# Attention: the causal mask of the transposed scores, by matrix products or by a selection on GpSimd

## The chip, the cores and the metric

The kernel runs on one core of one Trainium2 chip. The metric is the device time of one execution in microseconds (us). Before the change three runs gave 3653.22, 3657.49 and 3666.11 us; the median is 3657.49 us.

## The reference, cut to what matters

The whole program is a two-layer network on 16 sequences of 512 tokens with 128 features. The change touches one part of layer 0, where two attentions run on the same normalised input: A, without a causal mask (with a decay by distance), and B, causal. Both have 16 heads of 8 features. For B:

```python
scores = jnp.einsum('bhqd,bhkd->bhqk', q, k) / jnp.sqrt(jnp.float32(HD))
causal = jnp.tril(jnp.ones((s, s), dtype=bool))
scores = jnp.where(causal, scores, -jnp.inf)
attn = jax.nn.softmax(scores, axis=-1)
y = jnp.einsum('bhqk,bhkd->bhqd', attn, v)
```

The heads' outputs go on to a projection, a mixture of experts and a second layer, which the change does not touch.

## The kernel before, in words

`program` runs its stages one after the other: `fold_weights` (loads and reshapes weights), `front` (normalisation and projections), `attend` (both attentions of all heads), `tail`, `route`, `experts`, then layer 1. Only `fold_weights` and `attend` are changed.

`attend` works on 16 x 16 = 256 heads, one per step of a loop written out in full, and in groups of four heads. Keys come in four blocks of 128 (j = 0 to 3), queries are 512 wide. For each head there are three families of score products on TensorE (PE):

- A0 to A3: the scores of attention A, transposed (keys on partitions, queries along the free dimension), 512 wide each (line 627). VectorE (DVE) multiplies the first (j+1) x 128 columns by a decay ratio, in place in PSUM (line 782); ScalarE (ACT) takes the exponential into `pA` (line 729).
- M0, M1, M2: the scores of attention B with queries on partitions (line 633; M0 has the two narrow blocks, M1 the 384 wide one, M2 the 512 wide one). DVE takes the causal maximum of every row (line 791). Once per group these maxima are transposed (job MT, line 676), negated by DVE (line 754), split into three bfloat16 parts by GpSimd (POOL, lines 609 to 612), and loaded by DMA as three more rows of the operand `bq`.
- T0, T1, T2: the scores of attention B, transposed, eight steps after M (LAG = 8), because they need the maxima (line 640; T0 has key block 0, 512 wide; T1 has blocks 1 and 3, 384 and 128 wide; T2 has block 2, 256 wide). Behind each of the four products a second one, of the identity with `cmaskT`, adds -1e30 above the diagonal of the block's first 128 columns (line 643). ACT takes the exponential into `pB` (line 735), which has six slots.

Once per group the values are multiplied in: PV of A has four chunks, one for each key block (eight matmul records per chunk, 512 wide), PV of T has chunks 0 (512 wide), 1 (384 wide) and 2 with 3 (256 and 128 wide together) (line 659). ACT then copies the sum from PSUM (`copy`, line 718), PE transposes it (jobs OT, line 672), and DVE divides by the softmax sum (lines 762 and 764).

What sets the order: three hand-written sequences, one for each engine, in which every step's work is issued.

```python
BANK = dict(A0=2, A1=4, A2=0, A3=1, M0=5, M1=4, M2=3, T0=5, T1=3, T2=2)
PE_ORDER = ("T0", "M2", "A0", "at0", "A1", "A3", "T1", "at1", "M0", "A2", "T2", "at2", "M1")
ACT_ORDER = (("copy", 1), ("T1", 1), ("T2", 1), ("A3", 1), ("A2", 1), ("copy", 0), ("T0", 0), ("A0", 0), ("A1", 0))
DVE_ORDER = ("M2", "A0", "A1", "job", "A3", "M0", "A2", "M1")
```

The number in `ACT_ORDER` says how many steps late ACT does the piece. Two score families share each PSUM bank but two (bank 0 for A2, bank 1 for A3), and a product waits until the bank's previous occupant has been read (`free_bank`, line 616). The once-a-group work goes into the places at0, at1 and at2 of PE's order. A planner (lines 495 to 513) puts it there by a number q counted from the first step e of a group (e divisible by 4): q goes to step e + q // 3, place at(q mod 3). Before: PV of T at q = 2, 3, 4, its transpose at 9; PV of A at 7, 8, 10, 12, its transpose at 17 (which is place at2 of step 1 of the next group); MT at 2. In the texts "step 0" to "step 3" are the steps with e mod 4 = 0 to 3. The PSUM bank of the values is copied by ACT in the same step if the last chunk was at at0 ("copy", 0) and first thing in the next step if it was at at1 or at2 ("copy", 1).

Of the kernel before, what the change touches and what calls it, by code (L numbers as in the profile page):

```python
# [18 lines left out]
BF16 = mybir.dt.bfloat16  # L19
I32 = mybir.dt.int32  # L20
U32 = mybir.dt.uint32
ALU = mybir.AluOpType
# [3 lines left out]
P = 128  # L26
NB, S, D = 16, 512, 128
# [11 lines left out]
MASKED = -1e30  # L39
# [19 lines left out]
def fold_weights(nc, c, W):  # L59

    with ExitStack() as ctx:
        sb = lambda n, s, d=F32: ctx.enter_context(nc.sbuf_tensor(n, s, d))
        sem = lambda n: ctx.enter_context(nc.semaphore(n))
        wk, wv, wsum, wsumT = sb("fw_k", [P, D]), sb("fw_v", [P, D]), sb("fw_s", [P, D]), sb("fw_sT", [P, D])
        wd, wuk, wuv = sb("fw_d", [P, 32]), sb("fw_uk", [32, D]), sb("fw_uv", [32, D])
        bT = sb("fw_bT", [32, D])
        wqkv, wqkv_g, g1 = sb("fw_qkv", [P, 3 * D]), sb("fw_qkv_g", [P, 3 * D]), sb("fw_g1", [P, 1])
        wq, cmaskT = sb("fw_q", [P, D]), sb("fw_cmaskT", [P, P])
        ps = ctx.enter_context(nc.psum_tensor("fw_ps", [P, 4, 512], F32))
        s_in, s_sum, s_pe, s_cp = sem("fw_in"), sem("fw_sum"), sem("fw_pe"), sem("fw_cp")  # L70
        block = ctx.enter_context(nc.Block())
        loads = [(wk, c["Wk"]), (wv, c["Wv"]), (wd, c["Wdown"]), (wuk, c["Wuk"]), (wuv, c["Wuv"]),
                 (wqkv, c["Wqkv"]), (g1, c["g1"]), (wq, c["Wq"]), (W["woA"], c["WoA"]), (W["woB"], c["WoB"]),
                 (W["ident"], c["ident"]), (W["hsum"], c["hsum"]), (cmaskT, c["cmaskT"]),
                 (W["ratio"], c["ratio"]), (W["cmask"], c["cmask"]), (W["g2b"], c["g2b"]), (W["wr"], c["Wr"])]

        by_head = lambda ap: ap.rearrange("p (h d) -> p h d", d=HD)
        by_feature = lambda ap: ap.rearrange("p (d h) -> p h d", d=HD)

        @block.sync  # L80
        def _(sp):
            for dst, src in loads:
                sp.dma_start(dst[:], src).then_inc(s_in, 16)

        @block.vector
        def _(dve):
            dve.wait_ge(s_in, 16 * len(loads))
            dve.tensor_tensor(wsum[:], wk[:], wv[:], ALU.add).then_inc(s_sum, 1)

            dve.tensor_scalar(wqkv_g[:], wqkv[:], g1[:, 0:1], None, ALU.mult).then_inc(s_sum, 1)  # L90
            dve.tensor_copy(by_feature(W["wqA"][:]), by_head(wq[:]))
            dve.tensor_copy(W["ident_bf"][:], W["ident"][:])
            dve.tensor_copy(W["cmaskT"][:], cmaskT[:])
            dve.memset(W["mhalf"][:], -0.5)
            dve.wait_ge(s_sum, 2)
            dve.tensor_copy(W["wB"][:, 2 * D:3 * D], wqkv_g[:, 2 * D:3 * D])
            for t in range(2):
                src = by_head(wqkv_g[:, t * D:(t + 1) * D])
                dve.tensor_copy(by_feature(W["wB"][:, t * D:(t + 1) * D]), src)

                pairs = src.rearrange("p h (n two) -> p h n two", two=2)
                dst = by_feature(W["wB"][:, (3 + t) * D:(4 + t) * D]).rearrange("p h (n two) -> p h n two", two=2)
                dve.tensor_copy(dst[:, :, :, 0], pairs[:, :, :, 1])
                dve.tensor_copy(dst[:, :, :, 1], pairs[:, :, :, 0])
            dve.wait_ge(s_pe, 1)
            dve.tensor_copy(wsumT[:], ps[:, 0, 0:D]).then_inc(s_cp, 1)
            dve.wait_ge(s_pe, 2)
            dve.tensor_copy(bT[:], ps[0:32, 1, 0:D]).then_inc(s_cp, 1)
            dve.wait_ge(s_pe, 4)
            dve.tensor_copy(by_feature(W["mk"][:]), by_head(ps[:, 2, 0:D]))  # L110
            dve.tensor_copy(W["mv"][:], ps[:, 3, 0:D]).then_inc(s_cp, 1)
            dve.wait_ge(s_cp, 3)

        @block.tensor
        def _(pe):
            pe.wait_ge(s_sum, 1)
            pe.transpose(ps[:, 0, 0:D], wsum[:], W["ident"][:]).then_inc(s_pe, 1)
            pe.wait_ge(s_cp, 1)

            pe.matmul(ps[0:32, 1, 0:D], wd[:], wsumT[:], start=True, stop=True).then_inc(s_pe, 1)  # L120
            pe.wait_ge(s_cp, 2)
            pe.matmul(ps[:, 2, 0:D], bT[:], wuk[:], start=True, stop=True).then_inc(s_pe, 1)
            pe.matmul(ps[:, 3, 0:D], bT[:], wuv[:], start=True, stop=True).then_inc(s_pe, 1)
# [296 lines left out]
def attend(nc, c, W, nb):  # L420
# [4 lines left out]
    with ExitStack() as ctx:  # L425
        sb = lambda n, s, d=F32: ctx.enter_context(nc.sbuf_tensor("at_" + n, s, d))
        sem = lambda n: ctx.enter_context(nc.semaphore("at_" + n))
# [22 lines left out]
        stored = [[sem(f"stored{a}{n}") for n in range(2)] for a in range(2)]  # L450
        filled, tilted, maxed, exped = (sem(n) for n in "filled tilted maxed exped".split())
        pv, ot_cp, job, job_read, m_ready = (sem(n) for n in "pv ot_cp job job_read m_ready".split())
        v_step, p_step, ones = (sem(n) for n in "v_step p_step ones".split())

        BANK = dict(A0=2, A1=4, A2=0, A3=1, M0=5, M1=4, M2=3, T0=5, T1=3, T2=2)
        PE_ORDER = ("T0", "M2", "A0", "at0", "A1", "A3", "T1", "at1", "M0", "A2", "T2", "at2", "M1")
# [41 lines left out]
        for e in range(0, STEPS):  # L498
            if e % 4 == 0 and e >= 4:
                if 0 <= (e - 4 - LAG) // 4 < GROUPS:  # L500
                    g = (e - 4 - LAG) // 4
                    for q, chunks in ((2, (0,)), (3, (1,)), (4, (2, 3))):
                        put(e, q, ("PV", "T", g, chunks))
                    put(e, 9, ("OT", "T", g))
                if (e - 4) // 4 < GROUPS:
                    g = (e - 4) // 4
                    for j, q in enumerate((7, 8, 10, 12)):
                        put(e, q, ("PV", "A", g, (j,)))
                    put(e, 17, ("OT", "A", g))
                    put(e, 2, ("MT", "M", g))  # L510
# [6 lines left out]
        jseq = {j: n for n, j in enumerate(jobs)}  # L517
        pvseq = {g: n for n, g in enumerate(pv_order)}
        LAST = 1 + max(e for (e, n), w in plan.items() if w)

        last_head = {"A": "A2", "T": "T2"}

        with nc.Block() as block:

# [69 lines left out]
            @block.gpsimd  # L594
            def _(pool):
                step = [0]

                def link(ins):

                    step[0] += 1  # L600
                    ins.then_inc(p_step, 1)
                    pool.wait_ge(p_step, step[0])

                for n in range(GROUPS):
                    b = n % 2
                    pool.wait_ge(job_read, jseq["MT", "M", n] + 1)
                    if n >= 2:
                        pool.wait_ge(m_in[(n - 2) % B_GROUPS], 48 * ((n - 2) // B_GROUPS + 1))
                    link(pool.tensor_copy(mrow[:, b, 0], neg[:, b]))  # L609
                    link(pool.tensor_tensor(res[:, b], neg[:, b], mrow[:, b, 0], ALU.subtract))  # L610
                    link(pool.tensor_copy(mrow[:, b, 1], res[:, b]))
                    pool.tensor_tensor(mrow[:, b, 2], res[:, b], mrow[:, b, 1], ALU.subtract).then_inc(m_ready, 1)

            @block.tensor
            def _(pe):
# [21 lines left out]
                def scores_t(kind, n):  # L637
                    slot = n // 4 % B_GROUPS
                    for j, col in T_BLOCKS[kind]:
                        pe.matmul(ps[:, BANK[kind], col:col + S - j * P], bk[:, slot, n % 4, j * P:(j + 1) * P], bq[:, slot, n % 4, j * P:S],  # L640
                                  start=True, stop=False)

                        ins = pe.matmul(ps[:, BANK[kind], col:col + P], W["ident_bf"][:], W["cmaskT"][:], start=False, stop=True)  # L643
                    ins.then_inc(filled, 1)

                def values(kind, g, chunks):
                    a, b = "AT".index(kind), g // NG
                    if chunks[0] == 0:
                        pe.wait_ge(v_in[b % 2], 32 * (b // 2 + 1))
                        pe.wait_ge(exped, nth["exped", (last_head[kind], 4 * g + 3)])  # L650
                        if pvseq[kind, g]:
                            pe.wait_ge(ot_cp, pvseq[kind, g])
                    for j in chunks:
# [1486 lines left out]
def weights(nc, ctx):  # L2140
# [2 lines left out]
                  ratio=[P, S], cmask=[P, S], hsum=[P, H], g2b=[P, D], wr=[P, E], mhalf=[P, 2 * NC],  # L2143
                  nmax=[H, 2 * NB])
    W = {n: sb(n, s) for n, s in shapes.items()}
    W["ident_bf"], W["cmaskT"], W["flag"] = sb("ident_bf", [P, P], BF16), sb("cmaskT", [P, P], BF16), sb("flag", [1, 1], I32)
    return W


def shape_constants():  # L2150
# [6 lines left out]
    cmask[:, S - P:] = np.where(np.arange(P)[None, :] <= np.arange(P)[:, None], 0.0, MASKED)  # L2157

    hsum = (np.arange(P)[:, None] % H == np.arange(H)[None, :]).astype(f32)
    cmaskT = np.where(np.arange(P)[:, None] <= np.arange(P)[None, :], 0.0, MASKED).astype(f32)  # L2160
    theta = (f32(10000.0) ** (f32(-2.0) * (np.arange(HD // 2, dtype=f32) / HD))).astype(f32)
    ang = (pos[:, None] * theta[None, :]).astype(f32)
    feature = np.arange(P) // H
# [22 lines left out]
    i, j = np.arange(P)[:, None] % SEG, np.arange(SEG)[None, :]  # L2186
    scan = dict(cos1=per_side(cos1), sin1=per_side(sin1), mask1=np.where(j <= i, 0.0, MASKED).astype(f32))
    return dict(**route, **scan, ident=np.eye(P, dtype=f32), decay=decay, ratio=ratio, cmask=cmask,
                hsum=hsum, cmaskT=cmaskT, rope=rope)


def inputs_of(a):
# [56 lines left out]
```

## Time and profile before

| | us |
|---|---|
| runs (three): median (lowest to highest) | 3657.49 (3653.22 to 3666.11) |
| the profiled execution, its own time | 3638.61 |
| its span from first to last instruction | 3636.5 |
| `attend`, first score product to last division | about 397 to 1600 |
| PE busy over the span | 2978.0 (82%) |
| DVE busy | 2830.2 (78%) |
| ACT busy | 1774.0 (49%) |
| POOL busy | 1734.2 (48%) |

The span covers all stages; shares of it say little of one stage. A PE matmul's record has a modelled end and overlaps its neighbours, so PE's work is read from the spacing of starts rather than from the busy share.

### The profile page before, as it was taken

How to read it: one execution, taken by the hardware profiler on the slowest of the kernel's cores; microseconds unless marked ns; L12 is line 12 of the kernel's file. 1: busy time of each engine (PE TensorE's matmuls, PEld its weight loads, DVE VectorE, ACT ScalarE, POOL GpSimd, SP SyncE). 2: the span in 40 equal slices, each digit the busy share in tenths (PEclk: the TensorE clock that was granted, in tenths of full speed). 3: DMA queues.
4: the chain of work that ended last, by engine and by line, in shares of the span. 5: the costliest groups of instructions: out<-in, count | busy, mean ns of one | idle time of the engine just before them, and what ended most of it. 6: DMA issues, size and time to landing. Idle time of an engine off the chain costs nothing. (4 is left out here: it accounts for less than half of the span.)

```text
span 3636.5 us, 134756 instructions
## 1 busy us (share of the span) xinstructions
PE 2978.0 (82%) x56132; PEld 1772.6 (49%) x56132; DVE 2830.2 (78%) x7779; ACT 1774.0 (49%) x3541; POOL 1734.2 (48%) x1622
## 2 busy tenths in 40 slices
PE   4554599999999999985054179999999999999999
PEld 2222133333333333355012057777777777777777
DVE  5777788888888888857883578888888888888886
ACT  2222477787888877751000044444444444444443
POOL 4555000000000000012004478888888888888886
PEclk9777699999999999997565589999999999999999
DMA  3444533333333333247001300000000000000000
GB/s 129 147 152 153 131 78 79 81 86 82 81 84 86 86 81 81 71 127 226 3 0 34 80 9 10 10 10 10 10 10 10 10 7 7 10 10 10 10 7 10
DMA packets 179124, 210.76 MB, mean 58 GB/s; under 512 B 28196, under 2 KB 139876, under 8 KB 178276
## 3 DMA queue, kind: packets, MB, share of 16 engines
q1 hardware_dynamic: 175972, 200.94, 20.0%
q8 instruction: 442, 7.24, 0.9%
q0 software_dynamic: 2560, 1.35, 0.3%
q14 instruction: 150, 1.23, 0.1%
HBM read 125.79 MB, written 75.63 MB: 55 GB/s over the span
## 5 line engine op out<-in xcount | busy, mean ns | idle before, releaser
L729 ACT ACTIVATE at_pA<-at_ps 128x512 f32<-128x512 f32 x1024 | 569.4, 608 | 134.0 <-DVE at_ps L782 133.3
L791 DVE CUSTOM_DVE_ANT_0 at_junk<-at_ps,w_cmask 128x512 f32<-128x512 f32 (+3 forms) x1024 | 462.3, 487 | 166.4 <-PE at_ps L633 166.4
L609 POOL CAST at_mrow<-at_neg 16x128 bf16<-16x128 f32 x64 | 18.0, 281 | 1106.6 <-DVE at_neg L754 1106.6
L782 DVE TENSOR_TENSOR at_ps<-at_ps,w_ratio 128x128 f32<-128x128 f32 (+3 forms) x1024 | 490.0, 493 | 65.5 <-PE at_ps L627 65.4
L2001 ACT ACTIVATE sc_ee<-sc_ps 128x512 f32<-128x512 f32 x256 | 153.1, 598 | 606.2 <-PE sc_ps L1856 602.0
L735 ACT ACTIVATE at_pB<-at_ps 128x512 f32<-128x512 f32 (+1 forms) x768 | 395.9, 539 | 75.9 <-PE at_ps L643 73.0
L1819 POOL TENSOR_TENSOR sc_rb<-sc_rb,v_sin 128x512 f32<-128x512 f32 x256 | 326.2, 1274 | 99.6 <-DVE sc_ra L2040 99.1
L627 PE MATMUL at_ps<-at_aq,at_ak 72*128 72x512 bf16 x1024 | 353.3, 388 | 3.2 <-DMA at_ak<-parts_scratch 2.8
L1856 PE MATMUL sc_ps<-sc_xT,v_wqkv 128*128 128x512 f32 x512 | 298.4, 666 | 50.1 <-DVE sc_ra L2040 48.7
L633 PE MATMUL at_ps<-at_bk,at_bq 72*128 72x512 bf16 (+3 forms) x1024 | 271.3, 307 | 57.0 <-DMA at_bk<-parts_scratch 35.8
L640 PE MATMUL at_ps<-at_bq,at_bk 75*128 75x512 bf16 (+3 forms) x1024 | 281.4, 301 | 18.7 <-DVE at_mx L791 17.7
L659 PE MATMUL at_ps<-at_pA,at_v 128*32 128x512 f32 x2048 | 275.5, 610 | 0.0
L1881 PE MATMUL sc_ps<-v_uu,sc_skN 32*64 32x65 f32 x8192 | 259.6, 226 | 4.8 <-issue 1.3
L1881 PEld LDWEIGHTS sc_ps<-v_uu,sc_skN 32*64 32x64 f32 x8192 | 223.0, 135 | 52.3 <-issue 46.3
L2050 DVE TENSOR_TENSOR v_mem<-v_mem,sc_ps 128x520 f32<-128x520 f32 x256 | 171.9, 672 | 66.3 <-PE sc_ps L1881 66.3
L633 PEld LDWEIGHTS at_ps<-at_bk,at_bq 72*128 72x128 bf16 x1024 | 80.1, 99 | 280.4 <-ACT at_pA L729 123.6
L643 PE MATMUL at_ps<-w_cmaskT,w_ident_bf 128*128 128x128 bf16 x1024 | 198.3, 219 | 0.0
L2039 DVE STREAM_SHUFFLE sc_rb<-sc_ps 128x512 f32<-128x512 f32 x256 | 187.6, 733 | 0.0
L1933 PE MATMUL sc_ps<-v_wout,sc_oT 128*128 128x128 f32 x1024 | 183.6, 303 | 0.6
L1814 POOL TENSOR_TENSOR sc_sq<-sc_ee,sc_relu 128x512 f32<-128x512 f32 x128 | 165.1, 1290 | 36.6 <-ACT sc_ee L2004 36.2
L1814 POOL TENSOR_TENSOR sc_sk<-sc_ee,sc_relu 128x512 f32<-128x512 f32 x128 | 163.0, 1273 | 35.9 <-ACT sc_ee L2004 35.2
L659 PE MATMUL at_ps<-at_pB,at_v 128*32 128x512 f32 (+3 forms) x2048 | 177.3, 442 | 1.3 <-issue 0.9
(299 smaller groups left out, 6620.4 us busy)
## 6 DMA issues: line engine op xcount, KB each, us to landing
parts_scratch<-fr_parts SPq DMA_DIRECT2D x64, 384.0 KB, 2.8
at_bq<-parts_scratch SPq DMA_DIRECT2D x192, 96.0 KB
at_bk<-parts_scratch SPq DMA_DIRECT2D x192, 96.0 KB
at_aq<-parts_scratch SPq DMA_DIRECT2D x192, 96.0 KB
at_ak<-parts_scratch SPq DMA_DIRECT2D x192, 96.0 KB
v_scratch<-fr_v SPq DMA_DIRECT2D x32, 352.0 KB, 2.3
at_v<-v_scratch SPq DMA_DIRECT2D x32, 352.0 KB, 3.6
parts_scratch<-fr_parts SPq DMA_DIRECT2D x32, 256.0 KB, 2.8
```

What stands on the lines that cost most here:

```text
L627: pe.matmul(ps[:, BANK[f"A{j}"], :], ak[:, slot, n % 4, j * P:(j + 1) * P], aq[:, slot, n % 4], start=True, stop=True).then_inc(filled, 1)
L633: ins = pe.matmul(ps[:, BANK[kind], col:col + wide], bq[0:ROWS, slot, n % 4, j * P:(j + 1) * P], bk[0:ROWS, slot, n % 4, 0:wide], start=Tr ...
L640: pe.matmul(ps[:, BANK[kind], col:col + S - j * P], bk[:, slot, n % 4, j * P:(j + 1) * P], bq[:, slot, n % 4, j * P:S], start=True, stop=F ...
L659: ins = pe.matmul(ps[32 * s:32 * s + 32, PV, q0:S], v[:, b % 2, a, j, h * (HD + 1):h * (HD + 1) + 32], probs, start=(j == 0), stop=(j == N ...
L729: act.activation(pA[:, n % A_RING, j * S:(j + 1) * S], src, ACT.Exp).then_inc(exped, 1)
L735: act.activation(pB[:, n % T_RING, at:at + wide], src[:, 0:wide], ACT.Exp).then_inc(exped, 1)
L782: dve.tensor_tensor(src[:, 0:wide], src[:, 0:wide], W["ratio"][:, S - wide:S], ALU.mult).then_inc(tilted, 1)
L791: ins = dve.tensor_tensor_reduce(junk[:, P * j * (j + 1) // 2:P * (j + 1) * (j + 2) // 2], src[:, col:col + wide], W["cmask"][:, S - wide: ...
L1814: pool.tensor_tensor(sig[which][:, p % 4], ee[:, n % 2], relu[:, n % 2], ALU.add).then_inc(G["sg"], 1)
L1819: pool.tensor_tensor(by_pos(rb[:, n % 2]), by_pos(rb[:, n % 2]), table("sin", which), ALU.mult).then_inc(G["sn"], 1)
L1856: pe.matmul(ps[:, bank_of("qk"[which], p), :], V["wqkv"][:, col:col + P], xT[:, p // PAIRS % 2], start=True, stop=True).then_inc(G["pj"], 1)
L1881: ins = pe.matmul(ps[64 * hh:64 * hh + 64, 4 + f % 2, g * VE:(g + 1) * VE], skN[32 * f:32 * f + 32, p % 4, g, 64 * hh:64 * hh + 64], uu[32 ...
```

## The change

It leaves out the four identity products per head, and the constant `cmaskT` with its load and two casts. After the exponentials of T1 and T2 have been taken, POOL sets to 0, in `pB`, the entries whose query index within the diagonal block is below the key index: one selection over 128x128 (block 3) after T1 and one over three 128x128 blocks (0, 1 and 2) after T2, for each head. PE's products of the values wait for a new semaphore, `cut`, in place of the exponential. The planner's places of PV of T move from q = 2, 3, 4 to 3, 4, 5, and its transpose from 9 to 10. POOL's splitting of the maxima is now issued between the selections.

```diff
-            dve.tensor_copy(W["ident_bf"][:], W["ident"][:])
-            dve.tensor_copy(W["cmaskT"][:], cmaskT[:])
...
-                    for q, chunks in ((2, (0,)), (3, (1,)), (4, (2, 3))):
+                    for q, chunks in ((3, (0,)), (4, (1,)), (5, (2, 3))):
                         put(e, q, ("PV", "T", g, chunks))
-                    put(e, 9, ("OT", "T", g))
+                    put(e, 10, ("OT", "T", g))
...
-                for n in range(GROUPS):
+                def split_max(n):
...
+                def cut_future(n):
+
+                    probs = pB[:, n % T_RING]
+                    pool.wait_ge(exped, nth["exped", ("T1", n)])
+                    lone = probs[:, B_AT[3]:B_AT[3] + P]
+                    pool.affine_select(lone, lone, [[1, P]], ALU.is_ge, 0.0, base=0, channel_multiplier=-1).then_inc(cut, 1)
+                    pool.wait_ge(exped, nth["exped", ("T2", n)])
+                    three = bass.AP(probs.tensor, probs.offset, [list(probs.ap[0]), [S, 3], [1, P]])
+                    pool.affine_select(three, three, [[0, 3], [1, P]], ALU.is_ge, 0.0, base=0, channel_multiplier=-1).then_inc(cut, 1)
+
+                for e in range(STEPS):
+                    n = head_of("T", e)
+                    if n is not None:
+                        cut_future(n)
+                    if e % 4 == 0 and 0 <= e // 4 - 1 < GROUPS:
+                        split_max(e // 4 - 1)
...
                     for j, col in T_BLOCKS[kind]:
-                        pe.matmul(ps[:, BANK[kind], col:col + S - j * P], bk[:, slot, n % 4, j * P:(j + 1) * P], bq[:, slot, n % 4, j * P:S],
-                                  start=True, stop=False)
-
-                        ins = pe.matmul(ps[:, BANK[kind], col:col + P], W["ident_bf"][:], W["cmaskT"][:], start=False, stop=True)
+                        ins = pe.matmul(ps[:, BANK[kind], col:col + S - j * P], bk[:, slot, n % 4, j * P:(j + 1) * P], bq[:, slot, n % 4, j * P:S],
+                                        start=True, stop=True)
...
-                        pe.wait_ge(exped, nth["exped", (last_head[kind], 4 * g + 3)])
+                        if a == 0:
+                            pe.wait_ge(exped, nth["exped", ("A2", 4 * g + 3)])
+                        else:
+                            pe.wait_ge(cut, 2 * (4 * g + 3) + 2)
```

## Rows read from the trace of the kernel before

**Rows 1.** Busy time of a stretch of `attend`: PE, PEld, DVE, ACT, POOL, clock, DMA.
```profile
900.00:1000.00 100.00, 96.92 (x743) 39.31 (x744) 81.22 (x291) 80.39 (x165) 7.42 (x21) 1.00 0.31 74
```

**Rows 2.** Waits between 500 and 1500 us: total us, times, longest us.
```profile
PEld at_ps L627 <- DVE at_mx L791: 99.2, 162, 0.8
...
ACT at_oT L718 <- PE at_ps L659: 61.3, 108, 0.9
```

**Rows 3.** PE in time over one group: start us, us, what, [idle before <-releaser].
```profile
882.16 0.38 PE L640 MATMUL at_ps<-at_bq,at_bk 75*128 75x512 bf16 x1
...
883.61 0.34 PE L640 MATMUL at_ps<-at_bq,at_bk 75*128 75x384 bf16 x1
...
886.88 0.38 PE L640 MATMUL at_ps<-at_bq,at_bk 75*128 75x512 bf16 x1
...
891.06 0.38 PE L640 MATMUL at_ps<-at_bq,at_bk 75*128 75x512 bf16 x1 [0.28 <-DVE at_mx L791]
891.28 0.22 PE L643 MATMUL at_ps<-w_cmaskT,w_ident_bf 128*128 128x128 bf16 x1
891.34 0.38 PE L633 MATMUL at_ps<-at_bk,at_bq 72*128 72x512 bf16 x1
891.55 0.38 PE L627 MATMUL at_ps<-at_aq,at_ak 72*128 72x512 bf16 x1
891.86 1.07 PE L659 MATMUL at_ps<-at_pA,at_v 128*32 128x512 f32 x8
892.86 0.60 PE L627 MATMUL at_ps<-at_aq,at_ak 72*128 72x512 bf16 x2
...
894.13 0.34 PE L633 MATMUL at_ps<-at_bk,at_bq 72*128 72x128 bf16 x2 [0.33 <-ACT at_pB L735]
...
896.17 0.38 PE L640 MATMUL at_ps<-at_bq,at_bk 75*128 75x512 bf16 x1
...
898.63 0.86 PE L659 MATMUL at_ps<-at_pB,at_v 128*32 128x256 f32 x16
899.42 0.34 PE L633 MATMUL at_ps<-at_bk,at_bq 72*128 72x128 bf16 x2
...
899.99 0.61 PE L672 MATMUL at_ps<-w_ident,at_oT 128*128 128x128 f32 x4
900.43 0.33 PE L633 MATMUL at_ps<-at_bk,at_bq 72*128 72x384 bf16 x1
900.60 0.38 PE L640 MATMUL at_ps<-at_bq,at_bk 75*128 75x512 bf16 x1
```

**Rows 4.** ACT in time, the same group.
```profile
892.99 0.59 ACT L718 COPY at_oT<-at_ps 128x512 f32<-128x512 f32 x1 [0.91 <-PE at_ps L659]
893.48 0.60 ACT L735 ACTIVATE at_pB<-at_ps 128x512 f32<-128x512 f32 x1
...
899.56 0.59 ACT L718 COPY at_oT<-at_ps 128x512 f32<-128x512 f32 x1 [0.25 <-PE at_ps L659]
```

**Rows 5.** DVE in time, the same group.
```profile
890.49 0.42 DVE L791 CUSTOM_DVE_ANT_0 at_junk<-at_ps,w_cmask 128x256 f32<-128x256 f32 x1
890.83 0.09 DVE L791 DVE_READ_ACCUMULATOR2_ANT at_mx<- 128x1 f32 x1
...
893.63 0.24 DVE L762 RECIPROCAL at_rr<-at_ps 128x16 f32<-128x16 f32 x1
...
894.12 0.69 DVE L782 TENSOR_TENSOR at_ps<-at_ps,w_ratio 128x512 f32<-128x512 f32 x1
894.71 0.28 DVE L791 CUSTOM_DVE_ANT_0 at_junk<-at_ps,w_cmask 128x128 f32<-128x128 f32 x1
```

**Rows 6.** POOL: groups by line and shape, busy us and mean ns.
```profile
L1819 POOL TENSOR_TENSOR sc_rb<-sc_rb,v_sin 128x512 f32<-128x512 f32 x256 | 326.2, 1274 | 99.6 <-DVE sc_ra L2040 99.1
...
L226 POOL TENSOR_TENSOR fr_sc<-fr_sc,w_mhalf 128x8 f32<-128x8 f32 x8 | 13.4, 1671 | 0.7
...
L1518 POOL MEMSET v_mem<- 128x8320 f32 x1 | 7.0, 7039 | 0.0
```

More of the change, by code:

```diff
@@ L67, in fold_weights @@
         wqkv, wqkv_g, g1 = sb("fw_qkv", [P, 3 * D]), sb("fw_qkv_g", [P, 3 * D]), sb("fw_g1", [P, 1])
-        wq, cmaskT = sb("fw_q", [P, D]), sb("fw_cmaskT", [P, P])
+        wq = sb("fw_q", [P, D])
         ps = ctx.enter_context(nc.psum_tensor("fw_ps", [P, 4, 512], F32))
@@ L73, in fold_weights @@
                  (wqkv, c["Wqkv"]), (g1, c["g1"]), (wq, c["Wq"]), (W["woA"], c["WoA"]), (W["woB"], c["WoB"]),
-                 (W["ident"], c["ident"]), (W["hsum"], c["hsum"]), (cmaskT, c["cmaskT"]),
+                 (W["ident"], c["ident"]), (W["hsum"], c["hsum"]),
                  (W["ratio"], c["ratio"]), (W["cmask"], c["cmask"]), (W["g2b"], c["g2b"]), (W["wr"], c["Wr"])]
@@ L452, in attend @@
         pv, ot_cp, job, job_read, m_ready = (sem(n) for n in "pv ot_cp job job_read m_ready".split())
-        v_step, p_step, ones = (sem(n) for n in "v_step p_step ones".split())
+        v_step, p_step, ones, cut = (sem(n) for n in "v_step p_step ones cut".split())
         BANK = dict(A0=2, A1=4, A2=0, A3=1, M0=5, M1=4, M2=3, T0=5, T1=3, T2=2)
@@ L519, in attend @@
         LAST = 1 + max(e for (e, n), w in plan.items() if w)
-        last_head = {"A": "A2", "T": "T2"}
         with nc.Block() as block:
@@ L2145, in weights @@
     W = {n: sb(n, s) for n, s in shapes.items()}
-    W["ident_bf"], W["cmaskT"], W["flag"] = sb("ident_bf", [P, P], BF16), sb("cmaskT", [P, P], BF16), sb("flag", [1, 1], I32)
+    W["flag"] = sb("flag", [1, 1], I32)
     return W
@@ L2159, in shape_constants @@
     hsum = (np.arange(P)[:, None] % H == np.arange(H)[None, :]).astype(f32)
-    cmaskT = np.where(np.arange(P)[:, None] <= np.arange(P)[None, :], 0.0, MASKED).astype(f32)
     theta = (f32(10000.0) ** (f32(-2.0) * (np.arange(HD // 2, dtype=f32) / HD))).astype(f32)
@@ L2188, in shape_constants @@
     return dict(**route, **scan, ident=np.eye(P, dtype=f32), decay=decay, ratio=ratio, cmask=cmask,
-                hsum=hsum, cmaskT=cmaskT, rope=rope)
+                hsum=hsum, rope=rope)
 def inputs_of(a):
```

## The prediction

> **What bounds it now.** I began with the page's busy shares and its 40 slices, which set `attend` apart (about 397 to 1600 us), then took the stretch table for a hundred microseconds of it [rows 1]. There TensorE's granted clock is 1.00 of 2.4 GHz; DVE and ACT are busy 81 and 80 of 100 us, POOL 7. PE's 97 is modelled. So no engine is plainly full, and POOL has room. The wait table [rows 2] shows each engine waiting for another: PE for DVE's maxima (99.2 us in 1000), ACT's copy for PE's values (61.3 us, 108 times, thus twice in each of 54 groups). What bounds the stage is a chain that runs through three in-order engines and the shared PSUM banks, so I laid out one group in time.
>
> The T0 products open the steps: 882.16, 886.88, 891.06, 896.17, 900.60 [rows 3]. Step 2 takes 4.72 us, step 3 4.18, step 0 5.11, step 1 4.43: 18.44 us for four heads. Starts are spaced by the columns: a mask product takes 0.06 us (891.28 to 891.34), a 512-wide score 0.21 to 0.22, a chunk of values 1.00 (891.86 to 892.86), or 0.79 for T's chunks 2 and 3 (898.63 to 899.42; chunk 1 likewise), and a transpose job 0.44 (899.99 to 900.43). On ACT a 512-wide piece costs 0.49 (892.99 to 893.48) and is ready at 0.60 [rows 4]. On DVE A3 costs 0.59, and M0's maximum is ready at 890.92, whereupon PE's T0 starts at 891.06 [rows 5].
>
> Followed in time, PE is the chain from T1 of step 2 (883.61) to step 0, except for a DVE piece before 891.06. In step 0 the values of A end at 892.86, ACT copies at 892.99, takes T0's exponential from 893.48, and only then PE's M0 starts (894.13) [rows 3, 4]. PE carries it again to M0 at 899.42. From there to the T1 that corresponds to 883.61, 2.63 us, it is DVE: M0, A2, M1 and M2 in sequence.
>
> **Part 1: the mask products.** Sixteen per group go, each 0.058 us of PE. Eleven lie on the chain: T1's two in each of steps 1, 2 and 3, T0's one in steps 0, 1 and 3, T2's one in steps 0 and 2. The other five are covered: in step 0 T1's two by ACT's copy, in steps 1 to 3 T2, T0 and T2 by DVE. 11 x 0.058 = 0.64 us per group; 62 groups with both kinds of values make 40 us. This alone would be a gain. The page "TensorE: Matmul & The Clock Gate" of the Trainium skill, section Back-to-back issue gap, gives about 81 ns per 128-column product in a stream with weight loads; by that the gain would be 11 x 0.081 x 62 = 55 us. The measured spacing decides: 0.058.
>
> **Part 2: POOL's selections.** The trace has none. Nearest rows [rows 6]: a memset writes 8320 elements in 7.04 us, 0.85 ns each (lower bound: 512 elements and two starts of 0.1, 0.6 us per head); a two-input operation over 512 takes 1.27, about 2.1 ns each over a start of 0.2; the power over 8 elements takes 1.67, 183 ns each (upper bound, 94 us per head). A selection is plain streaming work, so I take the two-input row: 0.45 + 0.99 = 1.45 us per head, inside a step of 4.6. The last head's T2 exponential ends before step 0's T0 plus 0.1 us; its second selection is done by 1.2, and its values are asked for at 5.03 (below). It costs nothing up to about 4.4 us per head, where POOL, with 1.4 us per group for splitting the maxima, would fill the step. POOL's splitting waits behind the next group's first selection; its result is due a whole group later.
>
> **Part 3: the moved values.** PV of T goes from place at2 of step 0 and at0, at1 of step 1 to at0, at1, at2 of step 1. I lay the group out again, masks gone, counting from step 0's T0 (0.00), waits as in the code:
> - Step 0: A0 0.42, values A3 0.73 to 1.72, A1, A3, T1 2.15. ACT copies at 1.85, T0's exponential ends 2.94, M0 2.99. DVE divides (OT of T) until 2.99, A3 until 3.56, M0 until 4.20. T0 of the next step: 4.30. Before it was 5.11: PV T0 (1.0) is gone, and DVE sets the end.
> - Step 1: A0 4.73, values T0 5.03 to 6.02, A1, A3, T1 6.45, values T1 6.76 to 7.55, M0 7.55, A2, T2 7.94, OT of A 8.05, values T2 and T3 8.54 to 9.33, M1, next T0 9.50. It is PE throughout: 5.20 against 4.43.
> - Step 2: the sum is now ready at 9.33, after T2 rather than before M0, and ACT's sequence has the copy ahead of T1's exponential, which has been ready since 7.0. Copy 9.46, T1's exponential 9.95 to 10.55; M2 needs its bank: 10.60 (PE idle for 0.9). DVE's M2 is ready at 11.71, T1 11.77, values A0 12.08, M0 13.07, values A1 13.66 to 14.65, next T0 14.82. 5.32 against 4.72: before, the copy and the exponential were done while PE still did M0, A2, T2, OT, M1 and T0.
> - Step 3: at0 is empty, so A1 waits for DVE's M1 (15.65) and T1 for M2 (16.24). OT of T 16.50, values A2 17.00 to 17.99, M0, DVE ready 19.01, next T0 19.15. 4.33 against 4.18.
>
> Sum: 4.30 + 5.20 + 5.32 + 4.33 = 19.15 against 18.44, 0.71 more. So the move costs 0.71 + 0.64 = 1.35 per group and gives back more than the masks bring. 62 x 0.71 = 44 us. At the start one DMA issue (0.47) and two casts (0.3) go; at the end the last values come a place later, about 1 us: nothing in all.
>
> The sum stands against the profiled execution's own 3638.61 us (span 3636.5): 3682.6. That execution was 18.9 us faster than the median 3657.49, to which the forecast refers: 3657.5 + 44 = **3701.5 us**.
>
> **Rivals.**
> - *The masks decide* (faster): ACT and DVE have slack of a fifth, and if my copy-and-exponential stall at step 2 is absorbed, 0.64 per group is won: 3657.5 - 40 = 3617. It turns at a cost of the move of 0.64 us per group. For: equal work moved within one group, POOL idle. Against: rows 3 and 4 show just this stall, 1.27 us from the end of values to M0, wherever a copy stands before an exponential that PE needs. 0.17.
> - *Gain and cost cancel*: the move costs about 0.64, half of what I laid out: 3657 give or take 11. 0.13.
> - *POOL becomes the bound*: beyond 4.4 us per head. At 5.0 a step is 5.0 + 0.35 = 5.35 instead of 4.61, on some 250 steps +185 us: 3842. For: POOL's rows span 0.85 to 183 ns per element. Against: 2.1 for everything streamed. 0.05. The page "GPSIMD Engine Reference", section Elementwise — side-by-side cycle accounting, says that data-dependent branching costs about 12 cycles per element; at its 1.2 GHz that would be 5.1 us per head and this rival's case. The selection depends on position and not on data, and no row here shows that price.
> - *The change doesn't do what it says*: the selected entries, 128 columns from each block's start with index below the partition's, are exactly those that `cmaskT` covered, so the work left is the same; I give this nothing.
>
> **Numbers.** The forecast's case has 0.65. Its own range: each step of the layout may be off by 0.1 to 0.15, 0.5 per group, so 0.2 to 1.3 per group, 3670 to 3738. For 8 in 10 I go down to 3630, which takes in the cancelling case and part of the faster one, and up to 3745; left out are most of the faster rival, POOL's case, and a tail. What a measurement can tell from no change is 0.3%, 11 us. From the cases: faster 0.19, same 0.13, slower 0.68.
>
> **What would show it.** In the changed profile: mask rows gone; T0 spaced 4.3, 5.2, 5.3, 4.3; 52 groups in 1000 us; ACT's idle before the copies about 2.9 us per group (0.9 before A's, 2.0 before T's) against 1.2; PE's M2 in step 2 waiting for T1's exponential; selections of 0.4 and 1.0 us, POOL busy about 35 in 100, PE never waiting for `cut`; DVE durations unchanged. I am wrong if M2 in step 2 follows T0 at once, if POOL's spacing per head passes 4 us, or if values of T start late behind `cut`.

## The result, and the profile after

The changed kernel takes 3716.83 us in the median of four runs (3710.63 to 3725.30), the kernel before 3655.35 in four; the ratio is 1.0166, with a 95% interval of 1.0131 to 1.0201. So it is 61 us slower; 3701.5 was forecast, in a range of 3630 to 3745.

The span of the profiled execution went from 3636.5 to 3709.5 us, 73 more. The work in `attend` went from 397.4 to 1599.8 us (first score product to the end of the last division) before, and from 395.6 to 1663.8 after: 1202.4 became 1268.3, 66 of the 73. What remains lies outside `attend`, in stages that the change does not touch but for the load and the two casts left out at the start. They took 2434.1 us of the span before and 2441.2 after; in the other profiles of this study they took between 2431 and 2453, so it is read as scatter.

First the stretch table of the changed kernel, with the columns of [rows 1] (PE, PEld, DVE, ACT, POOL, clock, DMA), over the same hundred microseconds:

```profile
900.00:1000.00 100.00, 91.69 (x623) 30.22 (x624) 77.16 (x277) 76.98 (x158) 23.84 (x62) 1.00 0.35 86
```

POOL went from 7 to 24 busy microseconds in 100, and PE, DVE and ACT all do less per microsecond than before: 277 DVE records against 291 (PE's fall also holds the mask products that are gone). The stage slowed as a whole, no engine became full, and the granted clock is still 1.00, the 2.4 GHz level. The groups of POOL in `attend` (busy us, mean ns) show why POOL is not the reason:

```profile
L618 POOL TENSOR_SCALAR_AFFINE_SELECT at_pB<-at_pB 128x384 f32<-128x384 f32 x256 | 133.3, 521 | 64.4 <-ACT at_pB L749 64.3
...
L615 POOL TENSOR_SCALAR_AFFINE_SELECT at_pB<-at_pB 128x128 f32<-128x128 f32 x256 | 74.8, 292 | 748.4 <-ACT at_pB L749 748.4
```

Together 0.81 us per head where 1.45 was taken, and inside a step of 4.8. It is POOL that waits, for ACT's exponentials. The waits between 500 and 1500 us, of which [rows 2] show two before:

```profile
ACT at_oT L732 <- PE at_ps L673: 144.5, 103, 2.6
PEld at_ps L646 <- ACT at_pB L749: 141.0, 155, 1.2
PEld at_ps L640 <- DVE at_mx L805: 110.7, 153, 0.8
```

ACT's idle before the copies of the value sums rose from 61.3 to 144.5 us, 2.8 per group (2.9 was expected). No product of values (L673) waits for a selection anywhere in the table. PE in time shows one group as the prediction laid it out; T0, 128x512 on line 653, opens each step:

```profile
901.25 0.39 PE L653 MATMUL at_ps<-at_bq,at_bk 75*128 75x512 bf16 x1
...
901.72 0.39 PE L640 MATMUL at_ps<-at_aq,at_ak 72*128 72x512 bf16 x1
902.04 1.07 PE L673 MATMUL at_ps<-at_pB,at_v 128*32 128x512 f32 x8
...
903.79 0.85 PE L673 MATMUL at_ps<-at_pB,at_v 128*32 128x384 f32 x8
904.58 0.34 PE L646 MATMUL at_ps<-at_bk,at_bq 72*128 72x128 bf16 x2
...
905.08 0.60 PE L686 MATMUL at_ps<-w_ident,at_oT 128*128 128x128 f32 x4
905.61 0.86 PE L673 MATMUL at_ps<-at_pB,at_v 128*32 128x256 f32 x16
906.40 0.34 PE L646 MATMUL at_ps<-at_bk,at_bq 72*128 72x384 bf16 x1
906.58 0.38 PE L653 MATMUL at_ps<-at_bq,at_bk 75*128 75x512 bf16 x1
907.68 0.39 PE L646 MATMUL at_ps<-at_bk,at_bq 72*128 72x512 bf16 x1 [0.72 <-ACT at_pB L749]
...
908.86 0.39 PE L653 MATMUL at_ps<-at_bq,at_bk 75*128 75x384 bf16 x2
...
911.95 0.38 PE L653 MATMUL at_ps<-at_bq,at_bk 75*128 75x512 bf16 x1
...
913.62 0.61 PE L686 MATMUL at_ps<-w_ident,at_oT 128*128 128x128 f32 x4
914.15 1.07 PE L673 MATMUL at_ps<-at_pA,at_v 128*32 128x512 f32 x8
...
916.32 0.38 PE L653 MATMUL at_ps<-at_bq,at_bk 75*128 75x512 bf16 x1 [0.34 <-DVE at_mx L805]
...
920.61 0.39 PE L653 MATMUL at_ps<-at_bq,at_bk 75*128 75x512 bf16 x1
```

And ACT around the long wait:

```profile
903.99 0.60 ACT L743 ACTIVATE at_pA<-at_ps 128x512 f32<-128x512 f32 x1 [0.35 <-DVE at_ps L796]
906.54 0.59 ACT L732 COPY at_oT<-at_ps 128x512 f32<-128x512 f32 x1 [1.95 <-PE at_ps L673]
907.02 0.88 ACT L749 ACTIVATE at_pB<-at_ps 128x512 f32<-128x512 f32 x2
```

Step by step, from T0 to T0 (before from [rows 3]):

| | before | laid out | measured |
|---|---|---|---|
| step 0 | 5.11 | 4.30 | 4.29 |
| step 1 | 4.43 | 5.20 | 5.33 |
| step 2 | 4.72 | 5.32 | 5.37 |
| step 3 | 4.18 | 4.33 | 4.37 |
| group | 18.44 | 19.15 | 19.36 |

ACT idles 1.95 us for T's sum, whose last product comes only after OT and just before M1; T1's exponential follows at 907.02; and PE's M2, whose bank T1 held, starts at 907.68, 1.10 after T0 where products go at 0.21 to 0.25. A group takes 0.92 us more than before.

### The profile page after: what moved, and what is told of

It reads as the page before. It is cut to its first block and busy times, and to the rows that moved or that the text cites. A ratio compares the mean times of both kernels' runs of the same rounds, so it can differ in the third digit from the quotient of the medians.

```text
span 3709.5 us, 133219 instructions
## 1 busy us (share of the span) xinstructions
PE 2987.7 (81%) x55108; PEld 1694.3 (46%) x55108; DVE 2829.3 (76%) x7777; ACT 1774.4 (48%) x3541; POOL 1939.1 (52%) x2134
## 3 DMA queue, kind: packets, MB, share of 16 engines
q0 software_dynamic: 2560, 1.35, 0.3%
## 5 line engine op out<-in xcount | busy, mean ns | idle before, releaser
L743 ACT ACTIVATE at_pA<-at_ps 128x512 f32<-128x512 f32 x1024 | 579.4, 615 | 109.8 <-DVE at_ps L796 108.6
L615 POOL TENSOR_SCALAR_AFFINE_SELECT at_pB<-at_pB 128x128 f32<-128x128 f32 x256 | 74.8, 292 | 748.4 <-ACT at_pB L749 748.4
L749 ACT ACTIVATE at_pB<-at_ps 128x512 f32<-128x512 f32 (+1 forms) x768 | 404.4, 551 | 58.2 <-PE at_ps L653 45.9
L653 PE MATMUL at_ps<-at_bq,at_bk 75*128 75x512 bf16 (+3 forms) x1024 | 269.2, 304 | 26.5 <-DVE at_mx L805 20.8
L673 PE MATMUL at_ps<-at_pA,at_v 128*32 128x512 f32 x2048 | 277.2, 613 | 0.0
L673 PE MATMUL at_ps<-at_pB,at_v 128*32 128x512 f32 (+3 forms) x2048 | 179.9, 447 | 1.2 <-issue 1.2
L640 PEld LDWEIGHTS at_ps<-at_aq,at_ak 72*128 72x128 bf16 x1024 | 80.5, 99 | 204.1 <-DVE at_mx L805 139.6
```

The costliest lines, as they stand in the source:

```text
L640: pe.matmul(ps[:, BANK[f"A{j}"], :], ak[:, slot, n % 4, j * P:(j + 1) * P], aq[:, slot, n % 4], start=True, stop=True).then_inc(filled, 1)
L673: ins = pe.matmul(ps[32 * s:32 * s + 32, PV, q0:S], v[:, b % 2, a, j, h * (HD + 1):h * (HD + 1) + 32], probs, start=(j == 0), stop=(j == N ...
L743: act.activation(pA[:, n % A_RING, j * S:(j + 1) * S], src, ACT.Exp).then_inc(exped, 1)
L749: act.activation(pB[:, n % T_RING, at:at + wide], src[:, 0:wide], ACT.Exp).then_inc(exped, 1)
```

## The experiments

Group times below are the distances of the first of POOL's splittings of the maxima, once per group. In the undisturbed stretches of a kernel nearly all of them agree to 0.02 us, so they resolve far more than the total time does. Each ratio is to runs of the kernel before that were taken beside the experiment; their medians lie between 3643 and 3655 us, so totals of different experiments are compared by their ratios.

**1. The selections without the move.** The changed kernel with

```diff
-                    for q, chunks in ((3, (0,)), (4, (1,)), (5, (2, 3))):
+                    for q, chunks in ((2, (0,)), (3, (1,)), (4, (2, 3))):
...
-                    put(e, 10, ("OT", "T", g))
+                    put(e, 9, ("OT", "T", g))
```

> The selections on POOL and no mask products, but the values of T and their transpose at their places of before (q = 2, 3, 4 and 9). Theory (the places cost, the masks bring): a group takes 18.44 - 0.64 = 17.8 us and the whole about 3655 - 40 = 3615 us. First rival (the selections or the wait for cut cost): the time stays near that of the changed kernel, 3717, and PE waits for POOL. Second rival (masks were covered): 3655.

Measured: 3609.63 us, ratio to before 0.9900 (0.9878 to 0.9921); group 17.79 to 17.80. The gain of 0.64 per group is, to 0.01, the eleven mask products on the chain times 0.058, and no value product waits for POOL:

```profile
915.19 0.38 PE L653 MATMUL at_ps<-at_bq,at_bk 75*128 75x512 bf16 x1 [0.34 <-DVE at_mx L805]
...
918.91 1.07 PE L673 MATMUL at_ps<-at_pB,at_v 128*32 128x512 f32 x8
```

The values of T start 3.72 us into step 0. POOL's last selection of that group (below) ends at 915.24 + 0.52 = 915.76, 3.15 us earlier. The old places had room for it.

```profile
915.24 0.52 POOL L618 TENSOR_SCALAR_AFFINE_SELECT at_pB<-at_pB 128x384 f32<-128x384 f32 x1 [0.43 <-ACT at_pB L749]
```

**2. The move without the selections.** The kernel before with the same lines of the planner changed the other way (2, 3, 4 to 3, 4, 5; 9 to 10).

> The kernel before, mask products and all, with only the places of T's values and transpose moved (q = 3, 4, 5 and 10). Theory: the move alone costs 1.35 to 1.55 us per group, so a group of 19.8 to 20.0 us and a time of 3655 + 84 to + 96, 3740 to 3750. Rival (the selections cost): near 3655.

Measured: 3743.66 us, ratio 1.0273 (1.0248 to 1.0298); group 19.93. The move costs 1.49 us per group with the masks and 19.36 - 17.80 = 1.56 without, where 1.35 was laid out. Here too the M2 of step 2 waits, with no selection in the program:

```profile
903.27 0.38 PE L640 MATMUL at_ps<-at_bq,at_bk 75*128 75x512 bf16 x1
903.49 0.22 PE L643 MATMUL at_ps<-w_cmaskT,w_ident_bf 128*128 128x128 bf16 x1
904.37 0.39 PE L633 MATMUL at_ps<-at_bk,at_bq 72*128 72x512 bf16 x1 [0.66 <-ACT at_pB L735]
```

The four corners now stand at 18.44 (neither), 17.80 (selections), 19.93 (move) and 19.36 (both).

**3. The stall itself.** The changed kernel, one entry of ACT's sequence moved:

```diff
-        ACT_ORDER = (("copy", 1), ("T1", 1), ("T2", 1), ("A3", 1), ("A2", 1), ("copy", 0), ("T0", 0), ("A0", 0), ("A1", 0))
+        ACT_ORDER = (("T1", 1), ("T2", 1), ("copy", 1), ("A3", 1), ("A2", 1), ("copy", 0), ("T0", 0), ("A0", 0), ("A1", 0))
```

> The changed kernel with one entry of ACT's sequence moved: the copy of a sum that ended at at1 or at2 comes behind T1's and T2's exponentials and no longer ahead of them. Theory (in step 2 the copy holds up T1's exponential, and that holds up PE's M2): step 2 loses the 0.9 us in which PE stands, 5.37 becomes about 4.5, a group 18.5, the time about 3717 - 55 = 3662. Rival (the long step 1 is what costs, the stall is slack): a group stays at 19.3, the time at 3717.

Measured: 3663.23 us, ratio 1.0051 (1.0032 to 1.0070); most groups 18.51. Step 2 lost its wait: T0, M2 and the A products follow at 0.22, and the step lasts 914.06 - 909.53 = 4.53 us instead of 5.37.

```profile
909.53 0.38 PE L653 MATMUL at_ps<-at_bq,at_bk 75*128 75x512 bf16 x1
909.75 0.38 PE L646 MATMUL at_ps<-at_bk,at_bq 72*128 72x512 bf16 x1
909.97 1.05 PE L640 MATMUL at_ps<-at_aq,at_ak 72*128 72x512 bf16 x3
...
914.06 0.38 PE L653 MATMUL at_ps<-at_bq,at_bk 75*128 75x512 bf16 x1
```

So 0.85 of the 1.56 us are that one copy ahead of T1's exponential.

**4. The transpose.** The changed kernel with `put(e, 9, ("OT", "T", g))` and the values left at 3, 4, 5.

> The changed kernel with only the transpose of T's sum back at place 9 (at0 of step 3), the values staying at 3, 4, 5. Theory (at place 9 the transpose ran while PE's A1 and T1 would wait for DVE anyway, at place 10 it is added behind T1): 0.36 us per group less, a group of 19.0 us, 3717 - 22 = 3695 us. Rival (only the values' move costs): a group of 19.36, 3717.

Measured: 3714.88 us, ratio 1.0170 (1.0150 to 1.0191): the total does not move. Yet most groups take the 19.0 us that were expected (18.99 to 19.00 in 47 of the 63 distances). But every seven of them are followed by two long ones, as these starts show (20.08 and 21.04 after 19.00):

```profile
948.00 0.28 POOL L605 CAST at_mrow<-at_neg 16x128 bf16<-16x128 f32 x1 [1.89 <-DVE at_neg L768]
967.00 0.28 POOL L605 CAST at_mrow<-at_neg 16x128 bf16<-16x128 f32 x1 [1.88 <-DVE at_neg L768]
987.08 0.28 POOL L605 CAST at_mrow<-at_neg 16x128 bf16<-16x128 f32 x1 [2.97 <-DVE at_neg L768]
1008.12 0.28 POOL L605 CAST at_mrow<-at_neg 16x128 bf16<-16x128 f32 x1 [1.89 <-DVE at_neg L768]
```

The stretch table (PE, PEld, DVE, ACT, POOL, clock, DMA) around the first of the two, and PE there:

```profile
978.00:983.00 5.00, 4.12 (x24) 1.28 (x22) 4.39 (x19) 3.81 (x9) 0.82 (x2) 1.00 0.57 143
984.00:990.00 6.00, 6.00 (x27) 1.80 (x28) 2.89 (x11) 2.10 (x5) 1.50 (x5) 0.50 0.23 50
```

```profile
983.89 1.94 PE L673 MATMUL at_ps<-at_pB,at_v 128*32 128x512 f32 x8
985.76 1.03 PE L640 MATMUL at_ps<-at_aq,at_ak 72*128 72x512 bf16 x2
```

TensorE's granted clock fell to 0.50, its 1.2 GHz level, for about 7 us; a chunk of values took 1.87 us from start to start where it takes 1.00. There are seven such falls before the stage's last 10 us; each pair of long groups costs 3.1 us (1.08 + 2.04), 22 us together, just what 62 x 0.36 had won. Nor is it only the profiled execution: all five runs of this kernel have a mean granted clock of 0.896 to 0.898, those of the changed kernel 0.902 to 0.907. What PE did before this fall is step 0 and the step before it, with waits of 0.34 and 0.45 us for DVE and ACT. The kernel before and experiments 1 and 2 have no fall in their steady groups. The changed kernel has one, which makes two distances of 20.34 and 19.96 out of 19.36 each. Experiment 3 has nine, eight of them among its steady groups, whose long distances make 14 us that its total would have gained otherwise. Why one kernel has many of these and another one or none was not tried.

**5. Both repairs, the values still moved.** Experiments 3 and 4 together.

> The changed kernel with both repairs: the copy of the step before behind T1's and T2's exponentials, and the transpose of T's sum back at place 9; only the values stay moved. Theory (the two parts of the move's cost add up): 19.36 - 0.85 - 0.36 = 18.15 us per group where TensorE's granted clock stays at its upper level, and 3640 us if it stays there throughout; each stretch at the lower level costs about 3 us, as in the two kernels before. Rival (they overlap): 18.4 to 18.5 per group.

Measured: 3640.12 us, ratio 0.9984 (0.9969 to 0.9999); groups 18.14 to 18.15 at the upper clock, with six falls among them (four cost 1.6 us each and two 3.1, where I had written 3). The parts add: 0.85 + 0.36 = 1.21. What is left of the move, 18.15 - 17.80 = 0.35, is the placing of T's values alone. The total meets the 3640 by luck: that figure was for a clock that never falls, and the runs of the kernel before that belong to this experiment are 12 us faster than the first four (3643.29 against 3655.35).

The steps, from T0 to T0 in the median, show where each part lies:

| | step 0 | step 1 | step 2 | step 3 |
|---|---|---|---|---|
| experiment 1, selections and old places | 4.99 | 4.18 | 4.61 | 4.00 |
| the changed kernel | 4.29 | 5.33 | 5.37 | 4.37 |
| experiment 3, copy later | 4.29 | 5.33 | 4.52 | 4.37 |
| experiment 4, transpose at 9 | 4.29 | 5.33 | 5.37 | 4.00 |
| experiment 5, both | 4.29 | 5.33 | 4.52 | 4.00 |

The copy costs only in step 2 and the transpose only in step 3; the values' move takes 0.70 off step 0 and 0.09 off step 2 and adds 1.15 to step 1.

**6. How much room the selections have.** Experiment 1 with every selection repeated, each waiting for the one before:

```diff
+                    for _ in range(3):
+                        link(pool.affine_select(lone, lone, [[1, P]], ALU.is_ge, 0.0, base=0, channel_multiplier=-1))
```

(and likewise for the three blocks; `range(5)` in the second kernel).

> sel_old_places with each selection done four times over (the three added ones change nothing in the result; each waits for the one before, 0.08 us). POOL's work per head goes from 0.8 to about 3.7 us, and the last one of a group ends some 3.1 us after step 0's T0, where the values ask for it at 3.7. Theory (covered up to 4.4 us per head): the time stays at that of sel_old_places, 3610, a group at 17.8. Rival (the selections already disturb the other engines, or the old places leave them too little room): some tens of us more.

> The same with six times each: 5.7 us per head, four heads and the splitting of the maxima 24 us per group against 17.8. Theory: POOL is now the bound, 6.3 us per group more, about 3610 + 390 = 4000 us. Rival (other slack takes it up): under 3700.

Measured: with four times each 3632.81 us, ratio 0.9954 (0.9939 to 0.9970); POOL is busy 792 of 1000 us, and the groups still take 17.79. The end of the stage is longer: from the last group's splitting to the end of the last division 35.3 us instead of 22.1, since there the steps hold only T's part and are shorter than POOL's 3.6 us per head. With six times each, 4128.94 us, ratio 1.1305 (1.1276 to 1.1334), in two runs. POOL's own spacing makes 5.47 us per head (next selection of the same kind, 905.60 to 911.07 to 916.53), and the groups take 24.7 to 26.3. The value products now stand still until 0.10 us after POOL's last selection for the group (921.53 + 0.52 = 922.05; the row itself names no releaser, only "issue"), and the clock falls with them:

```profile
921.53 0.52 POOL L622 TENSOR_SCALAR_AFFINE_SELECT at_pB<-at_pB 128x384 f32<-128x384 f32 x1
```

```profile
922.15 1.94 PE L677 MATMUL at_ps<-at_pB,at_v 128*32 128x512 f32 x8 [4.34 <-issue]
```

```profile
500.00:1500.00 1000.00, 836.57 (x4720) 277.61 (x4719) 584.36 (x2068) 588.63 (x1171) 803.93 (x2032) 0.77 0.25 60
```

I had expected 24 us per group, and so 4000 us. The mean granted clock of 0.77 fits the direction of the miss: behind the wait of 4.3 us the records run at the lower level, as the 1.94 us for a chunk shows, and POOL too is idle for a fifth of the time, in part for want of exponentials. So the price beyond the bound was higher here than POOL's time alone; how much of it the clock makes was not tried. The bound lies between 3.6 and 5.5 us per head. That agrees with the 4.4 of the prediction, and with the (17.8 - 1.4) / 4 = 4.1 that the same sum gives for this kernel's shorter group.

**7. What the stall suggests for the faster kernel.** Experiment 1 with ACT's copies later. First the one of the same step behind T0's exponential, and the other as in experiment 3:

```diff
+        ACT_ORDER = (("T1", 1), ("T2", 1), ("copy", 1), ("A3", 1), ("A2", 1), ("T0", 0), ("copy", 0), ("A0", 0), ("A1", 0))
```

> Selections on POOL, old places, and both of ACT's copies later: the one of the step before behind T1's and T2's exponentials, the one of the same step behind T0's. Theory: in step 0 T0's exponential no longer waits for the values of A to end, so M0 comes about 0.6 us sooner; 0.2 to 0.6 us per group under sel_old_places, a group of 17.2 to 17.6 us, 3580 to 3603 us. Rival (DVE's sequence or the values set step 0 as soon as ACT does not): no gain over sel_old_places, 3615.

Measured: 3581.19 us, ratio 0.9815 (0.9791 to 0.9839); group 17.30. Then further:

```diff
+        ACT_ORDER = (("T1", 1), ("T2", 1), ("A3", 1), ("A2", 1), ("copy", 1), ("T0", 0), ("A0", 0), ("copy", 0), ("A1", 0))
```

> sel_old_copies_late with both of ACT's copies moved on by two more, resp. one more piece: the one of the step before behind A2's exponential, the one of the same step behind A0's. Theory (T2's product in step 0 waited 0.24 us for A0's exponential): up to 0.2 us per group, a group of 17.1, 3570 us, unless T's values then wait for the copy; rival (they do, 0.1 to 0.3): 3581 to 3600.

Measured: 3571.97 us, ratio 0.9781 (0.9765 to 0.9798); group 17.16 to 17.17. It beats both kernels. In step 0 PE goes from T1 to M0 in 0.22 us, without a wait, where experiment 1 has one of 0.45. Experiment 1, then this one:

```profile
918.21 0.34 PE L646 MATMUL at_ps<-at_bk,at_bq 72*128 72x128 bf16 x2 [0.45 <-ACT at_pB L749]
```

```profile
916.96 0.38 PE L653 MATMUL at_ps<-at_bq,at_bk 75*128 75x384 bf16 x2
917.18 0.33 PE L646 MATMUL at_ps<-at_bk,at_bq 72*128 72x128 bf16 x2
917.34 0.38 PE L640 MATMUL at_ps<-at_aq,at_ak 72*128 72x512 bf16 x1
917.56 0.27 PE L653 MATMUL at_ps<-at_bq,at_bk 75*128 75x256 bf16 x1
917.87 1.06 PE L673 MATMUL at_ps<-at_pB,at_v 128*32 128x512 f32 x8
```

**8. The copies' order with the masks.** The kernel before with the last sequence.

> The kernel before, mask products, places and all, with only ACT's two copies later, as in sel_old_copies_later. Theory (the copies' order is worth the same with and without the masks, but T1's two products in step 0 are no longer covered by the copy): 17.17 + 13 x 0.058 = 17.9 us per group, about 3655 - 33 = 3622 us. Rival (the order only helps where the masks are gone): 18.44 and 3655.

Measured: 3607.64 us, ratio 0.9914 (0.9891 to 0.9937); group 17.83. So the order is worth 0.61 us per group with the masks and 0.63 without, and the selections are worth 0.64 and 0.66: the two gains add up to within 0.02.

## Why the prediction was right

**Part 1** held. Eleven of sixteen mask products on the chain at 0.058 us made 0.64 us per group, and experiment 1 measured 18.44 - 17.80. The rule of the Trainium skill, page "TensorE: Matmul & The Clock Gate", section Back-to-back issue gap, with 81 ns would have made it 0.89; the trace does not agree with it here, and the measured spacing decided.

**Part 2** held in what it said of the total, with a price mis-sized that does not enter it. The selections take 0.29 and 0.52 us, 0.81 per head rather than 1.45: 0.23 us for 256 more elements, thus 0.9 ns each over a start of 0.18, which is the memset's pace and not that of the two-input row that I chose. Nor did POOL's work slow DVE's: the 512-wide maximum takes 688 ns after and 689 before. The limit was tested by experiment 6.

**Part 3** held in its mechanism and was a little too small. 1.35 us per group was laid out, 1.56 measured. By step the misses are 0.13 in step 1, 0.05 in step 2, 0.04 in step 3 and 0.01 the other way in step 0. In step 1 three intervals account for it: A0 came 0.47 after T0 rather than 0.43, the chunk after OT at 0.53 rather than 0.49, and M0 3.33 after T0 rather than 3.25, which already holds the first. The named cause of the stall in step 2, ACT's copy ahead of T1's exponential, was shown by experiments 2 and 3: it appears with the move alone and goes with one entry of ACT's sequence, worth 0.85 of the 1.56. The waits in step 3 that the empty place opened were shown by experiment 4: with the transpose back in that place the step takes 4.00 again, as in experiment 1. The layout has 4.33 - 4.00 = 0.33 for this, and 0.36 was measured. The remaining 0.35 is step 1's excess over what steps 0 and 2 save.

**The sum** was 44 us and the medians say 61; the two profiles' `attend` says 66. 60 steady groups times 0.92 make 55, against the 44 of 62 times 0.71. The term "at the end about 1 us: nothing in all" was mis-sized as well. The first two group distances take 41.4 us instead of 37.1: the granted clock, at 0.50 from before the stage on, rises about 16 us later than before (the stretch 441 to 457 us is at 0.83 after and at 1.00 before). The end, from the last but one splitting on, takes 4.7 us more. With 1.6 us for the fall of the clock that makes 66. The stretch before, then after:

```profile
441.00:457.00 16.00, 15.36 (x120) 5.36 (x120) 12.32 (x44) 12.53 (x26) 0.65 (x2) 1.00 0.35 76
```

```profile
441.00:457.00 16.00, 15.11 (x77) 4.28 (x79) 11.68 (x41) 11.12 (x24) 2.80 (x7) 0.83 0.22 60
```

The late rise need not be the change's: in ten of the twelve profiles, two of them of kernels with mask products, the first two distances take 41.3 us or more, and only those of the kernel before (37.1) and of experiment 3 (37.9) are shorter. So these 4 us may belong to the one profiled execution of the kernel before; its cause was not tried. The falls of the clock among steady groups stood nowhere in the prediction: the changed kernel has one, worth 1.6 us, but as many as in experiment 4 would have made 22.

The range had a slip: 0.71 and 0.5 make 1.21 per group and not 1.3, so its own upper end is about 3733 us rather than 3738. The measured time is inside either.

**The rivals.** "The masks decide" and "Gain and cost cancel" fell by the move's cost, 1.56 and thus over twice the 0.64 at which gain and cost would have been equal; but the first had the right price for the change without the move. "POOL becomes the bound" fell at 0.81 us per head, and experiment 6 shows that it would have been a real one. The page "GPSIMD Engine Reference" of the Trainium skill, section Elementwise — side-by-side cycle accounting, has 12 cycles per element for data-dependent branching; nothing of that is in these rows, which have 0.9 ns per element.

## What to carry to other kernels

Taking work off an engine is worth only the pieces that stand on the chain, and those can be counted in one period of the timeline; moving other work "to be safe" must be costed with the same care, since here it gave back more than twice what was won. Where an engine runs in a fixed order, ask of each piece that waits for something late what stands ready behind it: ACT's copy, needed by nobody soon, held back an exponential that PE needed at once, and putting it later was worth as much as the whole replacement. Check the slack before making room for a new operation: POOL had 3 us where it was given another step.

## What the runs showed that I had not expected

TensorE's granted clock can fall in the midst of groups that are all alike. In experiments 3, 4 and 5, steady groups of 18.1 to 19.0 us with waits of PE of under 0.8 us in them are interrupted six to eight times by a few microseconds at the 1.2 GHz level, each costing some 1.6 to 3.1 us; experiment 4's whole gain of 22 us was lost in this way while the kernel's instructions did just what was expected. The falls come at even distances, 174.1 us in experiment 4 and mostly 112.6 us in experiment 3. The waits alone do not decide it: experiment 1 has the same two of 0.34 and 0.45 us in every group as experiment 3, and no such fall. A change of half a percent in such a kernel is read from its undisturbed periods first and from its total afterwards.
